# A three-stage graph network kernel: the root term of layer one moves from the prologue into the tiles of pass one, and the step tables are turned before they are written

## The chip, the cores and the metric

The kernel runs on one core of a Trainium2 chip. The metric is the device time of one execution in microseconds (us); lower is better. Engines are named as in the profile: PE is TensorE, DVE is VectorE, ACT is ScalarE, POOL is GpSimd, SP is SyncE. The names ending in q (SPq, ACTq) are an engine's own sequencer, here the rows in which it issues transfers.

## What is computed

There are 12500 nodes with rows of 128 floats and 400000 edges, sorted by destination. Cut to what matters:

```python
h = relu(layernorm(x))
# relational convolution, 10 relations, applied twice
def rgcn(h, w_rel, root, bias):
    mean = segment_sum(h[src], dst * 10 + edge_type) / max(count, 1)   # (N, 10, 128)
    return einsum('nrd,rdo->no', mean, w_rel) + h @ root + bias
x = x + rgcn(relu(rgcn(h, w_rel1, root1, b1)), w_rel2, root2, b2)
# attention of four heads over the same edges
h = relu(layernorm(x))
x = x + attention(h, src, dst, W_l, W_r, att, bias)
```

`edge_type` is the position of the largest of ten of the 42 attributes of an edge. The term `h @ root1 + b1` is called the root term of layer one below.

## The kernel before, in words

The program has four stages with a barrier of all engines after each of the first three: `prologue()`, pass one (`rgcn_pass("p1", True, NextRows)`), pass two (`rgcn_pass("p2", False, Attention)`) and `attention_pass()`. Nothing of a stage starts before the one ahead of it has ended on every engine.

**The prologue** works through the nodes in 15 blocks (`NB`), each of 7 tiles (`BT`) of 120 nodes (`TN`). For block b, ACT issues the load of x (420 KB) into one of two buffers (line 494), DVE takes mean and variance (`stats`, lines 376 to 386), ACT takes the root (503), DVE the inverse (`inverse`, 388 to 394), ACT writes seven normalized tiles (`rows`, 505 to 514), and SP stores them to the table `htab[0]` (line 328, 433 KB), which the gathers of pass one read. PE then turns the seven tiles (`turn`), multiplies each by `root1` and adds `b1` by a product of one row of ones (`product`, lines 571 to 580); ACT copies the turned tiles out of PSUM (`turned`) and the products into `A_all` (`out_rows`). Each engine takes its blocks in a fixed order that is written out by hand, so whatever stands in one block's turn on an engine delays the next block there.

Into the same blocks other work is set. DVE's `more(b)` (lines 448 to 474) runs after `inverse(b)` and ahead of `stats(b + 2)`: casts in blocks 1 and 2, `last_rows` in 3, three rounds of counting in 4, 5 and 6 (`counted`: 14, 9 and 6 passes over 625 numbers that PE has spread over the partitions, `spread`), the step tables in 7 (`tables`), and one quarter of the edge types of the first two chunks of edges in each of blocks 8 to 11 (`rels.part`). The attributes for the last two of these are loaded by SP in blocks 9 and 10 (lines 330 to 332); each such load is 1.3 MB in two transfers (line 224). PE's order is: `turn(b)`, `product(b - 1)`, and behind these the early turning of destinations and sources in blocks 2 and 3 (line 588), `spread` in 4, 5 and 6 (lines 596 and 597), and `rels.turn` in 10 and 12.

After block 14, SP writes the step tables to memory. They lie in SBUF with one step per partition and are wanted in step order, so each four-byte number is an element of its own in these nine writes (lines 335 to 342):

```python
sp.dma_start(qstep_dram[0:QPLANE].rearrange("(c p) -> p c", p=P), qtab[:, :]).then_inc(s_step, 16)
```

Two more writes follow, SP waits for all eleven (line 345), and five reads bring the tables back in rows and spread over the partitions (lines 347 to 350); the last is 896 KB. Then the stage can end.

**Pass one and pass two** run the same function. POOL gathers the source rows of 625 groups of 640 edges, five indirect transfers for a group (line 700), into ten slots. 1680 steps in 168 rounds of ten each match one group with one window of 12 nodes: DVE builds the one-hot matrix (797), PE multiplies (919), DVE adds to the running sum (853), SP writes the sum out (756). From round 64 on each round also finishes one tile of 120 nodes. For tile n, SP reads ten partial sums into `S` (line 745, one at each step of the round), DVE waits for them at step 2 of the next round (line 807) and divides by the counts, PE turns ten blocks of 120 x 128 (882), DVE copies them out (832, parts of 4, 4 and 2 tiles), PE multiplies by the ten relation matrices (902) and DVE adds the result to `A_all` (825). There are 105 tiles. In pass one `NextRows` then makes the rows of layer two, with its own root product (991, 996, 997). Five late rounds at the end finish the last tiles with no steps beside them.

**The attention stage** gathers again for 625 groups and isn't touched by the change.

Of the kernel before, what the change touches and what calls it, by code (L numbers as in the profile page):

```python
# [20 lines left out]
I32 = mybir.dt.int32  # L21
# [84 lines left out]
def build(nc, x, src, dst, attr, w_rel1, root1, b1, w_rel2, root2, b2, w_l, w_r, att, bias, out,  # L106
# [78 lines left out]
    with outer:  # L185
# [78 lines left out]
        def prologue():  # L264

            with ExitStack() as st:
# [16 lines left out]
                tab = sbuf(st, "tab", [P, 5, SCOLS], I32)  # L283
                tabf = sbuf(st, "tabf", [P, SCOLS])
                qtab = sbuf(st, "qtab", [P, QCOLS], I32)
                qtabf = sbuf(st, "qtabf", [P, QCOLS])
                wtab = sbuf(st, "wtab", [P, WCOLS], I32)
                wt = sbuf(st, "t1_w", [P, D])
                brow = sbuf(st, "t1_b", [1, D])
                xin = [sbuf(st, f"t1_x{k}", [TN, BT * D]) for k in range(2)]  # L290
# [4 lines left out]
                ht = [sbuf(st, f"t1_ht{k}", [P, 4 * TN]) for k in range(2)]  # L295
# [3 lines left out]
                pt = [bank[:, 1024 + k * 512:1024 + k * 512 + 4 * TN] for k in range(2)]  # L299
                py = [bank[0:TN, 2048 + k * 512:2560 + k * 512] for k in range(2)]  # L300
# [8 lines left out]
                s_eps, s_w = sem("t1_eps_set", True), sem("t1_w_in", True)  # L309
                s_x = [sem(f"t1_x_in{k}", True) for k in range(2)]  # L310
                s_st, s_var, s_std, s_rs = sem("t1_stats", True), sem("t1_variance", True), sem("t1_std", True), sem("t1_rstd", True)
                s_hn, s_t, s_ht = sem("t1_rows", True), sem("t1_turned", True), sem("t1_copied", True)
                s_m, s_y = sem("t1_product", True), sem("t1_out", True)
                s_out = [sem(f"t1_stored{k}", True) for k in range(2)]

                with nc.Block() as block:

                    @block.sync
                    def _(sp):
# [14 lines left out]
                        with nc.allow_non_contiguous_dma(reason="a column per 128 steps"):  # L334
                            sp.dma_start(qstep_dram[0:QPLANE].rearrange("(c p) -> p c", p=P), qtab[:, :]).then_inc(s_step, 16)
                            sp.dma_start(qstep_dram[QPLANE:].rearrange("(c p) -> p c", p=P), wtab[:, :]).then_inc(s_step, 16)
                            sp.dma_start(qbase_dram.rearrange("(c p) -> p c", p=P), qtabf[:, :]).then_inc(s_step, 16)
                            sp.dma_start(base_dram.rearrange("(c p) -> p c", p=P), tabf[:, :]).then_inc(s_step, 16)
                            sp.dma_start(attcol_dram.rearrange("(c p) -> p c", p=P), tab[:, 4, :]).then_inc(s_step, 16)
                            for k in range(4):  # L340
                                plane = step_dram[1].rearrange("s k -> (s k)")[k * PLANE:(k + 1) * PLANE]
                                sp.dma_start(plane.rearrange("(c p) -> p c", p=P), tab[:, k, :]).then_inc(s_step, 16)
                        sp.dma_start(qdone, done_q).then_inc(s_step, 16)
                        sp.dma_start(done_dram.rearrange("(a g) -> a g", a=1), done_t[:, :]).then_inc(s_step, 16)
                        sp.wait_ge(s_step, 176)
                        for k, to in enumerate((qgroup, qlast)):
                            sp.dma_start(to, qstep_dram[k * QPLANE:k * QPLANE + to.shape[1]].rearrange("(a s) -> a s", a=1)).then_inc(s_step, 16)
                        sp.dma_start(attcol, attcol_dram.rearrange("(a s) -> a s", a=1)).then_inc(s_step, 16)
                        sp.dma_start(base[:, :], base_dram.rearrange("(a s) -> a s", a=1).to_broadcast([P, PLANE])).then_inc(s_step, 16)
                        sp.dma_start(qbase[:, :], qbase_dram.rearrange("(a s) -> a s", a=1).to_broadcast([P, QPLANE])).then_inc(s_step, 16)  # L350
                        sp.wait_ge(s_step, 256)
                        for k in range(2):
                            sp.wait_ge(s_out[k], 16 * ((NB + 1 - k) // 2))

# [12 lines left out]
                    def _(dve):  # L367
# [8 lines left out]
                        def stats(b):  # L376

                            k = b % 2
                            dve.wait_ge(s_x[k], 16 * (b // 2 + 1) + (16 if b == NB - 1 else 0))
                            if b >= 2:  # L380
                                dve.wait_ge(s_hn, b - 1)
                            for q in range(BT):
                                v.bn_stats(stat[k][:, q, :], xin[k][:, q * D:(q + 1) * D]).then_inc(s_st, 1)
# [40 lines left out]
                        def tables():  # L424

                            link(v.tensor_scalar(gs[:, :], gs[:, :], float(GROUPS - 1), None, ALU.min))
                            link(v.tensor_tensor(qtabf[:, :], snum[:, :], gs[:, :], ALU.subtract))
                            link(v.tensor_scalar(qtabf[:, :], qtabf[:, :], float(KW), None, ALU.mult))
# [1416 lines left out]
```

## Time and profile before

| | us |
|---|---|
| median of 3 runs | 12420.08 |
| lowest and highest | 12411.02, 12423.86 |
| profiled execution, its own time | 12413.02 |
| its span, first to last instruction | 12411.2 |

| engine | busy us | share of the span |
|---|---|---|
| PE | 9026.6 | 73% |
| PEld | 8216.0 | 66% |
| DVE | 7740.8 | 62% |
| ACT | 2071.1 | 17% |
| POOL | 8996.3 | 72% |

The shares are averages over four stages. The stages are told apart by POOL: it gathers in the two passes and in the attention stage, and stands still in the prologue and around each barrier. A duration such as "2.80" beside x7 is that of seven instructions merged into one row. PE's rows count the pieces of a product: a float32 product of two matrices is two records.

### The profile page before, as it was taken

What the parts mean: (1) busy time and instruction counts of PE and PEld (TensorE: products, weight loads), DVE (VectorE), ACT (ScalarE), POOL (GpSimd) and SP (SyncE); (2) the same over time, 40 slices, a digit from 0 to 9 for tenths busy, and PEclk for the clock granted to TensorE, in tenths of its full rate; (3) what the DMA queues carried; (4) which work ended last, traced back from release to release, by engine and by line L of the source; (5) the groups of instructions that cost most, each with busy time, mean ns of one, the idle gap of its engine ahead of it and who ended that gap; (6) DMA issues with size and microseconds to landing.
All of it is one profiled execution on the core that took longest, in us unless ns stands there. A gap on an engine that the chain in (4) does not pass through costs nothing. (4 is left out here: it accounts for less than half of the span.)

```text
span 12411.2 us, 236943 instructions
## 1 busy us (share of the span) xinstructions
PE 9026.6 (73%) x59599; PEld 8216.0 (66%) x59599; DVE 7740.8 (62%) x17428; ACT 2071.1 (17%) x5955; POOL 8996.3 (72%) x9486
## 2 busy tenths in 40 slices
PE   5566667777777766666777777766777777777777
PEld 4566667777777666666777777765666666666666
DVE  2555545666666655544777777764666667666677
ACT  2000000000000000000000000014444444444442
POOL 0677777777777677777777777757777777777776
PEclk6777888889889888888899899888988999999998
DMA  3666545555555444444555555557888888888887
GB/s 70 136 137 138 111 82 112 114 114 114 113 113 115 101 82 81 82 82 88 115 117 117 116 116 117 117 114 194 237 234 237 233 237 236 235 236 234 235 236 206
DMA packets 1434213, 1831.89 MB, mean 148 GB/s; under 512 B 379591, under 2 KB 998431, under 8 KB 1426692
## 3 DMA queue, kind: packets, MB, share of 16 engines
q0 software_dynamic: 300000, 634.20, 28.0%
q1 hardware_dynamic: 910830, 881.77, 26.6%
q10 hardware_dynamic: 222113, 300.75, 7.8%
q8 instruction: 581, 9.52, 0.3%
q14 instruction: 689, 5.64, 0.2%
HBM read 1355.30 MB, written 458.67 MB: 146 GB/s over the span
## 5 line engine op out<-in xcount | busy, mean ns | idle before, releaser
L700 POOL DMA_INDIRECT p_g<-htab,p_i x6250 | 5915.8, 947 | 1966.7 <-issue 1890.8
L919 PE MATMUL p_pg<-p_g,p_oh 128*120 x33600 | 4855.1, 309 | 1828.1 <-ACTq L726 1497.1
L919 PEld LDWEIGHTS p_pg<-p_g,p_oh 128*120 128x120 f32 x33600 | 4596.0, 214 | 2052.6 <-issue 2035.5
L1293 POOL DMA_INDIRECT a_g<-xlw,a_i x3125 | 2987.3, 956 | 1036.0 <-issue 876.1
L797 DVE SCALAR_TENSOR_TENSOR p_oh<-key,qbase,p_cols 128x600 f32<-128x600 f32 x3370 | 2800.8, 831 | 13.9 <-issue 13.9
L853 DVE SCALAR_TENSOR_TENSOR p_acc<-p_acc,cont,p_pg 120x129 f32<-120x129 f32 x3360 | 1165.8, 347 | 2591.3 <-PE p_pg L919 2370.0
L717 ACT ACTIVATE p_i<-src_i 128x5 int32<-128x5 int32 x1240 | 258.2, 208 | 7566.4 <-DMA p_g<-htab,p_i 6934.4
L1766 PE MATMUL a_px<-a_g,ident 128*128 x1450 | 736.2, 593 | 832.2 <-SPq L1348 784.0
L1755 PE MATMUL a_pg<-a_v,a_into 128*128 128x132 f32 x7000 | 974.0, 289 | 63.0 <-POOL a_v L1312 20.7
L1755 PEld LDWEIGHTS a_pg<-a_v,a_into 128*128 128x128 f32 x7000 | 908.2, 203 | 74.1 <-issue 36.3
L1766 PEld LDWEIGHTS a_px<-a_g,ident 128*128 128x128 f32 x1450 | 239.8, 207 | 913.8 <-issue 912.4
L1680 DVE TENSOR_TENSOR A<-a_pg,A 128x132 f32 x700 | 201.9, 288 | 942.6 <-PE a_pg L1755 910.0
L1772 PEld LDWEIGHTS a_px<-a_xr,a_onto 128*128 128x128 f32 x4350 | 715.9, 222 | 69.3
L1398 ACT ACTIVATE a_away<-a_dst,a_minus 128x640 f32 x727 | 602.8, 829 | 856.0 <-issue 328.9
L1689 DVE TENSOR_TENSOR a_relu<-a_relu,a_pcon 128x640 f32<-128x640 f32 x725 | 587.2, 810 | 251.4 <-ACT a_relu L1452 250.7
L1772 PE MATMUL a_px<-a_xr,a_onto 128*128 128x132 f32 x4350 | 713.9, 308 | 0.0
L1691 DVE TENSOR_REDUCE a_score<-a_relu 128x20 f32<-128x640 f32 x725 | 594.4, 820 | 25.1
L1451 ACT ACTIVATE a_relu<-a_px 128x384 f32<-128x384 f32 x725 | 352.5, 486 | 1457.5 <-PE a_py L1772 1444.8
L1531 DVE TENSOR_TENSOR a_into<-a_pcon,local 128x640 f32<-128x640 f32 x725 | 587.9, 811 | 8.0 <-issue 7.5
L1523 DVE TENSOR_TENSOR a_v<-a_xj,a_w 128x640 f32<-128x640 f32 x676 | 547.5, 810 | 70.3 <-issue 35.7
L902 PE MATMUL p_pt<-p_w,p_st 128*120 128x128 f32 x4200 | 533.8, 286 | 71.6 <-DVE p_st L832 71.6
L902 PEld LDWEIGHTS p_pt<-p_w,p_st 128*120 128x120 f32 x4200 | 510.4, 195 | 82.6 <-DVE p_st L832 81.9
(230 smaller groups left out, 7055.4 us busy)
## 6 DMA issues: line engine op xcount, KB each, us to landing
a_xj<-xjw ACTq DMA_DIRECT2D x725, 330.0 KB
xjw<-a_g SPq DMA_DIRECT2D x625, 330.0 KB
partial<-p_acc SPq DMA_DIRECT2D x3360, 60.5 KB
a_dst<-in_dst_dram SPq DMA_DIRECT2D x625, 320.0 KB
p_s<-partial SPq DMA_DIRECT2D x2100, 60.5 KB
p_g<-htab,p_i POOLq DMA_INDIRECT x6250
a_g<-xlw,a_i POOLq DMA_INDIRECT x3125
a_xr<-xrw ACTq DMA_DIRECT2D x728, 66.0 KB
```

The lines of the kernel that those rows point to most:

```text
L700: pool.indirect_dma_start(gath[:, (k * G + q) * W:(k * G + q + 1) * W], None, table, bass.IndirectOffsetOnAxis(ap=stage[k][:, q:q + 1], ax ...
L797: v.scalar_tensor_tensor(onehot[k][:, :].rearrange("p (t n) -> p t n", t=G), key_f[:, ds(within(gp1 * G - G, TILES - G), G)].rearrange("p ...
L853: v.scalar_tensor_tensor(acc[k][:, :], acc[(k - 1) % ALOOK][:, :], cont[0:KW, ds(s, 1)], pg[bank(c, k)], ALU.mult, ALU.add).then_inc(s_acc, 1)
L902: last = t.matmul(po, St[:, r * TN:(r + 1) * TN], wrel[:, r * D:(r + 1) * D], start=(r == 0), stop=(r == NREL - 1))
L919: last = t.matmul(pg[bank(c, k)], onehot[b][:, q * KW:(q + 1) * KW], gath[:, ds(to + q * W, W1)], start=(q == 0), stop=(q == G - 1))
L1293: pool.indirect_dma_start(gbuf[k][:, q * W:(q + 1) * W], None, xlw, bass.IndirectOffsetOnAxis(ap=stage[k][:, q:q + 1], axis=0)).then_inc(s ...
L1398: a.activation(away[:, :], dall[:, ds(at, GE)], ACT.Abs, bias=minus[:, ds(s, 1)]).then_inc(s_away, 1)
L1531: v.tensor_tensor(into[b][:, :].rearrange("p (t n) -> p t n", t=G), colp.rearrange("p (a n) -> p a n", a=1).to_broadcast([P, G, P]), local ...
L1691: v.tensor_reduce(score[at[0]][:, at[1] * G * H:(at[1] + 1) * G * H], L[to][:, :].rearrange("p (t c) -> p t c", c=C), AX, ALU.add).then_in ...
L1755: last = t.matmul(sums(j, b), into[b][:, q * P:(q + 1) * P], V[b][:, q * W:(q + 1) * W], start=(q == 0), stop=(q == G - 1))
L1766: t.matmul(px[b], ident[:, :], gath[:, ds(ring, HEADT * W)], start=True, stop=False)
L1772: last = t.matmul(to, onto[b][:, q * P:(q + 1) * P], xr[k % RING][:, :], start=False, stop=q in (HEADT - 1, G - 1))
```

## The change

- The prologue no longer turns its tiles, multiplies by `root1` or writes `A_all`. ACT, PE and their waits for each other in this work are gone (`turn`, `product`, `turned`, `out_rows`).
- PE's order in the prologue is now a plain list: the early turns, three times `spread`, the turning of the tables, two times `rels.turn`. ACT copies the early turns out after blocks 1 and 2 (2 and 3 before).
- x has three buffers in place of two. The first three loads are issued at the start, and the load of block b + 3 after `rows(b)`.
- All tables are made as float32 side by side in one tile `made` of 128 x 73. PE turns it once, DVE copies it out twice (as integers and as floats), and SP writes nine pieces with 512 bytes in a row each.
- These writes (`tables_out`) stand in SP's order after block 11's store, and the reads back (`tables_in`) after block 13's store. The attribute loads stand after the stores of blocks 10 and 11 in place of 9 and 10.
- In pass one each tile reads its own 120 rows of `htab[0]` (61 KB, one more transfer on SP, ahead of the ten), turns them as an eleventh block, and adds an eleventh product and the product of ones with `b1`. DVE's third copy is 360 columns wide in place of 240, its wait covers eleven transfers, and it copies the result to `A_all` in place of adding. `root1` and `b1` are loaded at the start of the pass. Pass two is as before.

The diff, cut to its core:

```diff
-                xin = [sbuf(st, f"t1_x{k}", [TN, BT * D]) for k in range(2)]
+                widths = (QCOLS, WCOLS, SCOLS, SCOLS, SCOLS, SCOLS, SCOLS, QCOLS, SCOLS)
+                starts = [sum(widths[:n]) for n in range(len(widths) + 1)]
+                made = sbuf(st, "made", [P, starts[-1]])
+                qtab, wtab, tab0, tab1, tab2, tab3, tab4, qtabf, tabf = (made[:, a:a + n] for a, n in zip(starts, widths))
+                lying_i = sbuf(st, "lying_i", [starts[-1], P], I32)
+                lying_f = sbuf(st, "lying_f", [starts[-1], P])
+                xin = [sbuf(st, f"t1_x{k}", [TN, BT * D]) for k in range(3)]
...
+                    def tables_out(sp):
+
+                        planes = step_dram[1].rearrange("s k -> (s k)")
+                        to = [qstep_dram[0:QPLANE], qstep_dram[QPLANE:], *(planes[k * PLANE:(k + 1) * PLANE] for k in range(4)),
+                              attcol_dram, qbase_dram, base_dram]
+                        sp.wait_ge(s_tab, 1)
+                        for n, one in enumerate(to):
+                            lying = lying_i if n < 7 else lying_f
+                            sp.dma_start(one.rearrange("(c p) -> c p", p=P), lying[starts[n]:starts[n + 1], :]).then_inc(s_step, 16)
+                        sp.dma_start(qdone, done_q).then_inc(s_step, 16)
+                        sp.dma_start(done_dram.rearrange("(a g) -> a g", a=1), done_t[:, :]).then_inc(s_step, 16)
...
-                            if b in (9, 10):
-                                sp.wait_ge(rels.s_used, b - 8)
-                                rels.fetch(sp, 1, b - 9)
-                        sp.wait_ge(s_tab, 1)
...
+                            if b in (10, 11):
+                                sp.wait_ge(rels.s_used, b - 9)
+                                rels.fetch(sp, 1, b - 10)
+                            if b == 11:
+                                tables_out(sp)
+                            if b == 13:
+                                tables_in(sp)
...
-                            v.engine_nop().then_inc(s_tab, 1)
+                            v.engine_nop().then_inc(s_seen, 1)
+                            dve.wait_ge(s_lie, 1)
+                            v.tensor_copy(lying_i[:, :], plying)
+                            v.tensor_copy(lying_f[:, :], plying).then_inc(s_tab, 1)
...
-                            k = b % 2
+                            k = b % 3
...
-                            if b >= 2:
-                                act.wait_ge(s_hn, b - 1)
+                            if b >= 3:
+                                act.wait_ge(s_hn, b - 2)
...
-                                act.wait_ge(s_t, 2 * (b - 1))
                                 act.wait_ge(s_out[k], 16 * (b // 2))
...
-                        for b in range(NB + 2):
-                            if b < NB:
-                                deviation(b)
-                                rows(b)
-                                if b + 2 < NB:
-                                    load_x(b + 2)
-                            if 1 <= b <= NB:
-                                turned(2 * b - 2)
-                                turned(2 * b - 1)
-                            if b >= 2:
-                                out_rows(2 * b - 4)
-                                out_rows(2 * b - 3)
+                        for b in range(NB):
+                            deviation(b)
+                            rows(b)
+                            if b + 3 < NB:
+                                load_x(b + 3)
+                            if b == 1:
+                                early_out(dst_f, 0)
                             if b == 2:
-                                early_out(dst_f, 0)
-                            if b == 3:
                                 early_out(src_i, len(early))
...
+                        pe.wait_ge(s_cast, 1)
+                        turn_early(dstc, 0)
+                        pe.wait_ge(s_cast, 2)
+                        turn_early(srcc, len(early))
+                        spread(0, finq)
+                        spread(1, lastw)
+                        spread(2, fint)
+                        pe.wait_ge(s_seen, 4)
+                        nc.tensor.transpose(plying, made[:, :], ident[:, :]).then_inc(s_lie, 1)
+                        pe.wait_ge(s_pa, 2 * len(early))
+                        rels.turn(pe, 0)
+                        rels.turn(pe, 1)
...
+                parts = NREL + (1 if first else 0)
...
+                        if first:
+                            sp.dma_start(wrel[:, NREL * D:], root1).then_inc(s_w, 16)
+                            sp.dma_start(brow, b1.rearrange("(a d) -> a d", a=1)).then_inc(s_w, 16)
...
+                            if k == 0 and first:
+                                sp.dma_start(own[odd], table[ds(n * TN, TN), 0:D]).then_inc(s_sr[odd], 16)
...
-                                gate(dve, "dve", (s_sr[odd], 16 * WT * half + 16 * WT))
+                                gate(dve, "dve", (s_sr[odd], 16 * parts * half + 16 * parts))
...
-                                v.tensor_tensor(to, to, po, ALU.add).then_inc(s_add, 1)
+                                if first:
+                                    v.tensor_copy(to, po).then_inc(s_add, 1)
+                                else:
+                                    v.tensor_tensor(to, to, po, ALU.add).then_inc(s_add, 1)
...
-                                for r in range(NREL):
-                                    last = t.matmul(po, St[:, r * TN:(r + 1) * TN], wrel[:, r * D:(r + 1) * D], start=(r == 0), stop=(r == NREL - 1))
+                                for r in range(parts):
+                                    last = t.matmul(po, St[:, r * TN:(r + 1) * TN], wrel[:, r * D:(r + 1) * D], start=(r == 0), stop=(r == NREL - 1 and not first))
+                                if first:
+                                    last = t.matmul(po, then.ones[0:1, 0:TN], brow, start=False, stop=True)
```

## Rows read from the trace of the kernel before

**Rows 1.** Timeline of POOL: first and last gather of pass one, first of pass two.
```profile
337.02 2.14 POOL L700 DMA_INDIRECT p_g<-htab,p_i  x1 [0.97 <-ACT p_i L713]
...
4252.38 0.95 POOL L700 DMA_INDIRECT p_g<-htab,p_i  x1 [0.30 <-issue]
4315.18 2.03 POOL L700 DMA_INDIRECT p_g<-htab,p_i  x1 [61.85 <-ACT p_i L713]
```

**Rows 2.** Waits of POOL, 330 to 4300 us: total us, times, longest us.
```profile
POOL p_g L700 <- ACT p_i L717: 7.9, 26, 0.3
```

**Rows 3.** Groups by line, prologue (0 to 336 us): busy us, mean ns, idle before.
```profile
L579 PE MATMUL t_psum<-t_b,ones 1*120 1x128 f32 x210 | 81.6, 490 | 0.0
L578 PE MATMUL t_psum<-t_w,t_ht 128*120 128x128 f32 x210 | 80.1, 485 | 1.2 <-ACT A L527 1.2
```

**Rows 4.** Timelines of ACT, PE and DVE in the prologue, put in order of time.
```profile
55.40 2.80 ACT L512 ACTIVATE t_h<-t_x,t_rs 120x128 f32<-120x128 f32 x7 [19.96 <-DMA htab<-t_h]
...
77.42 0.47 DVE L399 TENSOR_SCALAR key<-key 1x625 int32<-1x625 int32 x1
...
82.13 0.47 DVE L407 TENSOR_SCALAR done_t<-cont 1x625 int32<-1x625 f32 x1
...
92.77 5.11 PE L588 MATMUL t_psum<-ident,raw 125*128 125x125 f32 x24
...
116.83 0.87 DVE L414 TENSOR_SCALAR_CACHE_REDUCE qbase<-t_psum,snum 128x625 f32<-128x625 f32 x1 [17.48 <-PE t_psum L597]
...
129.68 1.46 DVE L383 BATCH_NORM_STATS2 t_st<-t_x 120x6 f32<-120x128 f32 x7
...
132.06 2.80 ACT L512 ACTIVATE t_h<-t_x,t_rs 120x128 f32<-120x128 f32 x7 [27.40 <-DVE t_rs L393]
...
185.44 0.17 DVE L426 TENSOR_SCALAR gs<-gs 128x14 f32<-128x14 f32 x1
...
194.69 0.17 DVE L445 TENSOR_SCALAR tab<-ring 128x6 int32<-128x6 f32 x1
...
197.28 0.82 DVE L237 TENSOR_REDUCE local<-local 125x64 f32<-125x640 f32 x1
...
200.86 0.20 DVE L248 TENSOR_SCALAR local<-local 125x64 f32<-125x64 f32 x1
...
211.18 0.36 ACTq L494 DMA_DIRECT2D t_x<-in_x_dram  x1
...
222.02 1.45 DVE L383 BATCH_NORM_STATS2 t_st<-t_x 120x6 f32<-120x128 f32 x7 [9.86 <-DMA t_x<-in_x_dram]
...
276.74 2.80 ACT L512 ACTIVATE t_h<-t_x,t_rs 120x128 f32<-120x128 f32 x7 [12.92 <-DVE t_rs L393]
...
281.86 2.80 ACT L512 ACTIVATE t_h<-t_x,t_rs 120x128 f32<-120x128 f32 x7 [0.47 <-DVE t_rs L393]
```

**Rows 5.** Timeline of SP's issues at the end of the prologue: start, us.
```profile
285.05 0.53 SPq L335 DMA_DIRECT2D qstep_dram<-qtab  x1
...
313.73 0.41 SPq L344 DMA_DIRECT2D done_dram<-done_t  x1
327.01 0.51 SPq L347 DMA_DIRECT2D tabs<-qstep_dram  x2
...
328.24 0.43 SPq L350 DMA_DIRECT2D qbase<-qbase_dram  x1
```

**Rows 6.** Windows: PE, PEld, DVE, ACT, POOL busy, PEclk, DMA share, GB/s.
```profile
80.00:100.00 20.00, 16.65 (x60) 12.22 (x60) 4.87 (x21) 6.58 (x15) 0.00 (x0) 1.00 0.18 44
100.00:132.00 32.00, 13.40 (x39) 9.03 (x39) 14.52 (x44) 4.17 (x11) 0.00 (x0) 0.51 0.11 27
```

**Rows 7.** Groups by line in the rounds with tiles, 2000 to 3600 us.
```profile
L902 PE MATMUL p_pt<-p_w,p_st 128*120 128x128 f32 x1380 | 176.2, 287 | 0.0
...
L882 PE MATMUL p_pt<-ident,p_s 120*128 120x120 f32 x680 | 103.7, 287 | 88.1 <-DVE A L825 52.8 <-DVE p_st L832 35.3
```

**Rows 8.** Waits of PE in the same stretch: total us, times, longest us.
```profile
PE p_pg L919 <- ACTq L726: 211.8, 126, 4.8
```

More of the change, by code:

```diff
@@ L298, in prologue @@
                 psf = bank[:, 0:1024]
-                pt = [bank[:, 1024 + k * 512:1024 + k * 512 + 4 * TN] for k in range(2)]
-                py = [bank[0:TN, 2048 + k * 512:2560 + k * 512] for k in range(2)]
+                plying = bank[0:starts[-1], 1024:1024 + P]
                 pz = [bank[:, 3072 + k * 512:3072 + k * 512 + 4 * CH] for k in range(2)]
@@ L343, in _ @@
[L343 to L348, printed above, removed]
@@ L378, in stats @@
                             k = b % 2
-                            dve.wait_ge(s_x[k], 16 * (b // 2 + 1) + (16 if b == NB - 1 else 0))
+                            dve.wait_ge(s_x[b % 3], 16 * (b // 3 + 1) + (16 if b == NB - 1 else 0))
                             if b >= 2:
@@ L559, in _ @@
                         t = nc.tensor
-                        def turn(p):
-                            b, n = p // 2, 4 if p % 2 == 0 else BT - 4
-                            pe.wait_ge(s_hn, b + 1)
-                            if p >= 2:
-                                pe.wait_ge(s_ht, p - 1)
-                            for q in range(n):
-                                at = 4 * (p % 2) + q
-                                last = t.transpose(pt[p % 2][:, q * TN:(q + 1) * TN], hb[b % 2][:, at * W:at * W + D], ident[0:TN, 0:TN])
-                            last.then_inc(s_t, 1)
-                        def product(p):
-                            n = 4 if p % 2 == 0 else BT - 4
-                            pe.wait_ge(s_ht, p + 1)
-                            if p >= 2:
-                                pe.wait_ge(s_y, p - 1)
-                            for q in range(n):
-                                to = py[p % 2][:, q * D:(q + 1) * D]
-                                t.matmul(to, ht[p % 2][:, q * TN:(q + 1) * TN], wt[:, :], start=True, stop=False)
-                                last = t.matmul(to, ones[0:1, 0:TN], brow[0:1, :], start=False, stop=True)
-                            last.then_inc(s_m, 1)
                         def turn_early(of, base_n):
@@ L881, in turn @@
                             for m, r in enumerate(which):
-                                last = t.transpose(to[:, m * TN:(m + 1) * TN], S[odd][:, r * W1:r * W1 + D], ident[0:TN, 0:TN])
+                                of = S[odd][:, r * W1:r * W1 + D] if r < NREL else own[odd]
+                                last = t.transpose(to[:, m * TN:(m + 1) * TN], of, ident[0:TN, 0:TN])
                             last.then_inc(s_t, 1)
@@ L894, in mean @@
                                 pe.wait_ge(s_cpy, 3 * n + 1)
-                                turn(odd, range(8, NREL), pT[0])
+                                turn(odd, range(8, parts), pT[0])
                             n, odd, half, here, later = tile_at(j, c, 2)
```

114 lines of the change are left out of this document (33 added, 81 removed).

## The prediction

> **What bounds the kernel now.** I first read POOL's timeline, because POOL alone tells the stages apart. Its first gather of pass one starts at 337.02 us, its last at 4252.38, and pass two's first at 4315.18 [rows 1]. Between the first two lie 3124 gathers, 1.25 us each. The waits say that nothing held POOL back in pass one: all its waits on ACT, which hands it free slots, come to 7.9 us, none over 0.3 [rows 2]. So pass one is bound by POOL's own pace, and whatever PE, DVE and SP do there is free as long as POOL isn't starved. The reader is to see a kernel of stages in series: a prologue of 337 us in which POOL stands still, a pass that POOL sets, and a tail of 4315.2 - 4253.3 = 61.9 us in which the last steps and tiles drain. Pass two and the attention stage aren't touched. The change can gain only in the first of these, and lose only in the second and third.
>
> Next the groups of the prologue. The root products take 210 and 210 records for 105 tiles, 81.6 + 80.1 = 161.7 us of PE [rows 3], 1.54 us a tile and 10.8 us a block of seven. They delay more than PE: the counting on DVE waited 17.48 us for a spread that stood behind them at 116.83 [rows 4]. Last the queue of SP. After block 14, nine writes of single numbers and two others run from 285.05 to 314.1, the reads back can start only at 327.01, and the first gather starts 10.0 us after that [rows 5, 1]. These 52 us are the prologue's end; both they and the PE work must go for the stage to get shorter.
>
> **Part one, the prologue.** With the products gone, its length is set by the hand-written order on DVE, ACT and SP. I follow it block by block with durations of before.
>
> The opening is bound by transfers: `rows(2)` started at 55.40, after 19.96 us of waiting for a store [rows 4]. The third load of x now stands beside these, 420 KB more; no row shows what it adds. Below: nothing, since it was loaded in that time anyway. Above: the 10.8 us that a load, a store and an attribute load took together (issued 211.18, used 222.02) [rows 4]. I take 2, as it is a fifth of those bytes: `rows(2)` from 57.4 to 60.2. Behind it ACT copies the turned sources out, as fast as PE turns them, 5.1 us (at 92.77) [rows 4], and only then takes the root of block 3. `inverse(3)` is at 66.5.
>
> From here DVE is the chain, because `more(b)` stands ahead of `stats(b + 2)`. One block's statistics and inverse take 132.06 - 129.68 = 2.4 us [rows 4]. `last_rows` takes 5.2 (82.13 + 0.47 - 77.42) [rows 4], giving 74.1 after the statistics. One pass of counting takes (129.68 - 116.83) / 14 = 0.92 us [rows 4]: 14, 9 and 6 of them are 12.9, 8.3 and 5.5 us, each with 2.4 behind it. The spreads run beside those 2.4 us. That is 74.1 + 26.7 + 7.2 = 108.0. The tables take 194.69 - 185.44 + 0.2 = 9.4 us [rows 4]. The new turn of 73 columns and two copies have no row; from below 0.3 (one turn and nothing else), from above a spread's 2.4 us with two handovers, 4; I take 1.5, nearest to a single turn and two small copies. With 2.4 behind: 121.3. A quarter of the edge types takes 200.86 - 197.28 + 0.2 = 3.8 us [rows 4]; blocks 8 and 9 end at 121.3 + 2 x 6.2 = 133.7, and `rows(10)` at 133.7 + 3.0 = 136.7.
>
> Now **two waits that weren't there**. The attributes for `more(10)` are issued after block 10's store, no longer a block ahead. DVE stands at them, with `stats(12)` and so `rows(11)` queued behind; SP's next store waits for that. The three transfers together took 10.8 us (211.18 to 222.02) [rows 4]. Each such block costs 10.8 + 3.8 + 2.4 + 3.0 = 20.0 us. Below, a transfer half as long makes it 15; above, 16 us of transfer makes it 25. `rows(12)` ends at 176.7. Block 13 adds 5.5 and block 14 the 5.1 us that lie between 276.74 and 281.86 [rows 4]: 182.2 and 187.3.
>
> The writes of the tables now stand ahead of block 12's store, eleven issues. The two that were rows already took some 0.4 us each (0.41 at 313.73) [rows 5], so some 5 us, beside DVE's second wait, where SP has nothing else to do; if that cover went, block 12's store would slip by them. The reads back are issued after block 13's store, at 182.5. Before, 10.0 us lay between their first issue and the first gather [rows 5, 1]; the last store now shares these, so 13. The last store itself, issued at 187.4, ends at about the same time. **The first gather starts at 195.5 in place of 337.0: -141.5 us.** PE's and ACT's other removed work is inside this; the two extra weight loads at the head of pass one lie ahead of no gather and cost nothing.
>
> One rule speaks against this part. The clock that was granted was 1.00 from 80 to 100 us and 0.51 from 100 to 132 [rows 6], so the lower clock came only late in the stage; I take full rate for the early turns and half for the spreads. The Trainium skill (TensorE: Matmul & The Clock Gate, "What's actually happening") says that half rate is the default and that activity releases it. By that rule the thinned-out PE would do the early turns at half rate, 5.1 us more, and the time would be 5 us above mine.
>
> **Part two, pass one.** Each tile gains one turn (103.7 / 680 = 0.15 us), one product (two records of 1380 in 176.2: 0.26) and one with the bias row, 0.26 again [rows 7]; at half rate that last is 0.78 (2 x 81.6 / 210) [rows 3]. So 0.7 us, at most 1.3, on PE, plus one issue on SP and a wider copy on DVE. A round is 3915 / 168 = 23.3 us, and PE waits for gathered groups 211.8 us in 1600, 3.1 a round [rows 8]. That idle time is the cover; 0.7 fits in it. If it were gone, 105 tiles would cost 74 us. In the tail there is no cover: five tiles finish behind the last gather at 0.7 us, **+3.5 us** (0 to 7). DVE's wait for eleven transfers in place of ten costs nothing, since the eleventh is issued first.
>
> **Sum.** 12413.0 - 141.5 + 3.5 = 12275.0 for the profiled execution. The median shown is 7.1 us above that execution, so on its footing 12282.1; I say 12282.
>
> **The rivals.**
> A, transfers take DVE's place. The opening is bound by them, three loads are pushed into it, and both attribute loads now stand exposed. If the opening slips by the full 10.8 and each attribute load by 10 more, the first gather is at 226 and the time 12313. For: DVE waited 9.86 us for x at 222.02 [rows 4]. Against: in 80 to 132 us the transfer engines were 11 to 18% busy [rows 6].
> B, the order hides less than I think: the blocks keep their pace because of some wait that I took for PE's, and only the prologue's end is cut. The nine writes fall away, 314 - 285 plus the 13 us to 327.01, some 42 us [rows 5]: 12420 - 42 = 12378. Against: the 17.48 us names PE.
> C, the tiles crowd pass one. PE's clock or the longer chain of turns and copies makes POOL wait now and then; half of the exposed 74 us gives 12319.
> D, **slower**: the tile's gate. DVE's wait at step 2 (line 807) also holds back the steps' sums and one-hots. If the eleventh transfer, or SP's queue with it, holds DVE up for more than the 3.1 us of slack plus 138 / 105 = 1.3, so 4.4 us a tile, the gain is lost. At 5.5 us it is 105 x 2.4 = 252 us: 12420 - 138 + 252 = 12534. For: one more issue on SP's queue, which also serves the sums. Against: no wait of DVE on a transfer stands among the long ones.
> E, the change doesn't do what it says, since DVE or transfers had their own reason for each wait: within 25 us of no change.
>
> **Chances.** Forecast 0.76, A 0.11, B 0.04, C 0.05, D 0.02, E 0.02. Faster by over 0.2% (25 us, about what can be told from no change) takes in the first four: 0.96; same 0.02; slower 0.02. The range: downwards both attribute waits at 15 us take 10 off, the opening at no cost 2, the tail 3.5, and the median's footing 7: 12260. Upwards the clock adds 5, the attribute waits 10, the tail 3.5, the tables' turn 2.5, and A and C reach up to 12320.
>
> **What would show it.** Right: first gather near 195; DVE waits of about 10 us before line 237 in blocks 10 and 11; no wait for PE longer than a spread; POOL's waits on ACT in pass one still below 20 us; 62 us of tail become 65. The prediction is wrong if the stretch from `rows(3)` to `rows(10)` isn't near 70 us, if a wait on x or a store takes over there, or if POOL shows gaps beyond 0.3 us in the tile rounds.

## The result, and the profile after

| | before | after |
|---|---|---|
| median | 12417.74 us (4 runs) | 12281.04 us (4 runs) |
| lowest, highest | 12411.02, 12423.86 | 12275.18, 12286.73 |
| profiled execution | 12413.02 | 12275.18 |

The ratio is 0.9891 (95% interval 0.988 to 0.9903): 136.7 us less. A later pair gave 0.9885 (0.9869 to 0.9902), 12276.59 against 12421.3. The forecast was 12282.

First POOL's timeline of the changed kernel (start, us, line, tile): the same three places as [rows 1].

```profile
195.41 2.13 POOL L653 DMA_INDIRECT p_g<-htab,p_i  x1 [0.98 <-ACT p_i L666]
...
4110.68 0.94 POOL L653 DMA_INDIRECT p_g<-htab,p_i  x1 [0.30 <-issue]
4178.97 2.04 POOL L653 DMA_INDIRECT p_g<-htab,p_i  x1 [67.34 <-ACT p_i L666]
```

The first gather comes 141.6 us sooner. From there to the last gather it is 3915.3 us, in the kernel before 3915.4. The idle time behind it is 67.3 us in place of 61.9. So the whole gain lies ahead of 195.41, and 5.5 us of it are given back in the tail. From pass two's first gather to the end it is 8094.4 us, 1.6 less than before, which the change doesn't explain. The sum, 141.6 + 0.1 - 5.5 + 1.6 = 137.8, is the difference of the two profiled executions.

The waits in the prologue, by the waiting instruction and what ended the wait: total us, times, longest. First DVE's two largest for a block in the kernel before (0 to 337 us), then the changed kernel (0 to 198 us).

```profile
DVE t_st L383 <- DMA t_x<-in_x_dram: 68.0, 9, 15.6
...
DVE qbase L414 <- PE t_psum L597: 52.4, 3, 17.5
```

```profile
ACT t_h L517 <- DVE t_rs L396: 81.8, 14, 17.3
...
ACT t_h L517 <- DMA htab<-t_h: 17.1, 1, 17.1
DVE t_st L386 <- ACT t_h L517: 15.4, 3, 9.7
DVE local L237 <- DMA local<-in_edge_attr_dram: 14.7, 1, 14.7
DVE local L237 <- DMA ea<-in_edge_attr_dram: 14.5, 1, 14.5
```

Three things are to be seen. DVE's three waits of 17.5 us for a spread (one of them stands in [rows 4]) have shrunk to 0.6 us in all. Its waits for x, 68.0 us before and more than the spreads cost, are down to 9.1, all of them ahead of 20 us; the prediction names only one of them (9.86 us). And two waits are there that the kernel before didn't have: DVE stands 14.7 and 14.5 us at the attribute loads of blocks 10 and 11. What they do to the rest shows in ACT's rows (line 517 is `rows(b)`), here blocks 9 to 14:

```profile
126.00 2.80 ACT L517 ACTIVATE t_h<-t_x,t_rs 120x128 f32<-120x128 f32 x7 [2.40 <-DVE t_rs L396]
...
132.12 2.80 ACT L517 ACTIVATE t_h<-t_x,t_rs 120x128 f32<-120x128 f32 x7 [2.52 <-DVE t_rs L396]
...
153.06 2.80 ACT L517 ACTIVATE t_h<-t_x,t_rs 120x128 f32<-120x128 f32 x7 [17.35 <-DVE t_rs L396]
...
173.57 2.80 ACT L517 ACTIVATE t_h<-t_x,t_rs 120x128 f32<-120x128 f32 x7 [16.30 <-DVE t_rs L396]
...
178.86 2.80 ACT L517 ACTIVATE t_h<-t_x,t_rs 120x128 f32<-120x128 f32 x7 [2.30 <-DVE t_rs L396]
...
182.32 2.80 ACT L517 ACTIVATE t_h<-t_x,t_rs 120x128 f32<-120x128 f32 x7 [0.47 <-DVE t_rs L396]
```

Blocks 9 and 10 are 6.1 us apart, the two behind the loads come 20.9 and 20.5 us after the block ahead of them. The end of SP's queue, the answer to [rows 5]: the writes take 4.6 us for eleven, issued at 158.69 beside DVE's second wait, and the reads back are out before the last store.

```profile
158.69 0.74 SPq L322 DMA_DIRECT2D qstep_dram<-lying_i  x2
...
162.85 0.41 SPq L324 DMA_DIRECT2D done_dram<-done_t  x1
...
182.05 1.49 SPq L330 DMA_DIRECT2D tabs<-qstep_dram  x2
...
184.64 0.42 SPq L333 DMA_DIRECT2D qbase<-qbase_dram  x1
185.14 0.40 SPq L345 DMA_DIRECT2D htab<-t_h  x1
```

In pass one, the rounds with tiles (1860 to 3460 us): the groups by line that answer to [rows 7], with the new own turn and the bias product, and the wait that answers to [rows 8].

```profile
L864 PE MATMUL p_pt<-p_w,p_st 128*120 128x128 f32 x1518 | 186.6, 281 | 0.0
...
L866 PE MATMUL p_pt<-local,y_ones 1*120 1x128 f32 x138 | 32.7, 316 | 0.0
...
L844 PE MATMUL p_pt<-ident,local 120*128 120x120 f32 x68 | 19.3, 284 | 0.0
```

```profile
PE p_pg L883 <- ACTq L679: 159.4, 93, 4.9
```

The root term's own records are 19.3 us for the turn, 186.6 / 11 = 17.0 for the product and 32.7 for the bias in 68 or 69 tiles, together 1.0 us a tile. PE waits for gathered groups 52.4 us less, 0.77 us a tile, so the term is paid out of that idle time. The two numbers aren't the same thing: the mean granted clock of the stretch was 0.92 here and 0.89 in the kernel before, and the step products, which the change doesn't touch, took 931.5 us of PE in place of 957.2. POOL's waits on ACT for slots in the pass are 7.0 us, where they were 7.9.

### The profile page after: what moved, and what is told of

It is laid out like the page before. It is cut to its first block and busy times, and to the rows that moved or that the text cites. A ratio compares the mean times of both kernels' runs of the same rounds, so it can differ in the third digit from the quotient of the medians.

```text
span 12273.4 us, 236908 instructions
## 1 busy us (share of the span) xinstructions
PE 8873.7 (72%) x59600; PEld 8089.9 (66%) x59600; DVE 7757.1 (63%) x17430; ACT 2044.9 (17%) x5895; POOL 8995.7 (73%) x9486
## 5 line engine op out<-in xcount | busy, mean ns | idle before, releaser
L883 PEld LDWEIGHTS p_pg<-p_g,p_oh 128*120 128x120 f32 x33600 | 4544.3, 212 | 2026.4 <-issue 1997.2
```

Of the source, the lines that this page charges most:

```text
L883: last = t.matmul(pg[bank(c, k)], onehot[b][:, q * KW:(q + 1) * KW], gath[:, ds(to + q * W, W1)], start=(q == 0), stop=(q == G - 1))
```

## The experiments

Twelve runs of eleven kernels (one of them the changed kernel itself), in three sets, most of them with a single execution. The sets ran on different chips. On the chips of the first two sets the kernel before took 15981.29 us (one run) and 15948.28 (13 runs, 15906.29 to 15972.13); on the third 12421.3 (7 runs), as at first. The last section shows where the difference lies. The prologue is the same on all of them to about 1.5 us, so that the start of the first gather can be compared across the sets; times and pass one only within one.

**The order of the attribute loads.** `fetch_back`:

```diff
-                            if b in (10, 11):
-                                sp.wait_ge(rels.s_used, b - 9)
-                                rels.fetch(sp, 1, b - 10)
+                            if b in (9, 10):
+                                sp.wait_ge(rels.s_used, b - 8)
+                                rels.fetch(sp, 1, b - 9)
```

> The changed kernel with the attribute loads of the second chunk back behind the stores of blocks 9 and 10 (10 and 11 in the changed kernel). In the changed kernel DVE stands 14.7 and 14.5 us at them and the first gather starts at 195.4 us. Theory (the chain is DVE's order, and these two waits are on it): the first load can be issued about 6 us sooner against its use and the second a whole block sooner; the waits fall to about 8 and 2 us and the first gather starts near 176. Rival (transfers bound this stretch, whatever their order): the time comes back as waits on x or on stores, and the first gather stays above 190.

First gather at 177.14, 18.3 us sooner. DVE's waits in the prologue of this kernel:

```profile
DVE local L237 <- DMA local<-in_edge_attr_dram: 8.6, 1, 8.6
...
DVE local L237 <- DMA ea<-in_edge_attr_dram: 2.0, 1, 2.0
```

The two waits fell by 6.1 and 12.5 us, together 18.6, and all of that reached the first gather. In this stretch the chain is DVE's order, and transfers had room.

**The third buffer.** `two_buffers`: `range(3)` to `range(2)`, `b % 3` to `b % 2`, and the load of block b + 2 after `rows(b)`.

> The changed kernel with two buffers for x in place of three, all else as it is. Theory: where blocks are short (8 to 10) a load needs 5 to 6 us between rows(b) and stats(b + 2), which the third buffer hides; each of these blocks grows from 6 to about 11 us, block 14 by 5, the opening by 2 to 5, and the first gather starts near 218 in place of 195.4. Rival (DVE's other work hides the loads): 195 to 200.

First gather at 217.60, 22.2 us later than in the changed kernel. From 20 us on DVE now waits for x, where in the changed kernel it didn't:

```profile
DVE t_st L386 <- DMA t_x<-in_x_dram: 60.7, 8, 16.3
```

Counted from the start it is 69.0 us, against the changed kernel's 9.1. So the third buffer is worth 22 us, once the products are out of the way.

**The turned tables.** `tables_in_columns`, at the new place in SP's order:

```diff
-                            sp.dma_start(one.rearrange("(c p) -> c p", p=P), lying[starts[n]:starts[n + 1], :]).then_inc(s_step, 16)
+                                sp.dma_start(one.rearrange("(c p) -> p c", p=P), of).then_inc(s_step, 16)
```

> The changed kernel with the nine table writes as before, one number an element, at their new place behind block 11's store. Theory: SP needs some 28 us to issue them in place of 4, so block 12's store is issued at about 187 in place of 176.4, and the reads back wait for the writes until about 200; the first gather starts at 211 to 215 (195.4 in the changed kernel). Rival 1 (at their new place the writes are hidden, and the turning brought nothing): 195 to 200. Rival 2 (they cost all that they cost before, 41 us): 236.

First gather at 211.94, 16.5 us later. SP's queue in this kernel:

```profile
161.63 12.62 SPq L325 DMA_DIRECT2D step_dram<-made_i  x4
...
188.94 5.93 SPq L348 DMA_DIRECT2D htab<-t_h  x2
200.50 0.52 SPq L333 DMA_DIRECT2D tabs<-qstep_dram  x2
```

The writes take SP from 157.58 to 188.9, block 12's store waits behind them, and the reads back start at 200.50. At their new place the element-wise writes cost 16.5 us. Behind block 14, 42.0 us lie between the first write and the first read back (285.05 to 327.01), and with turned tables at that same place 6.6 (285.66 to 292.30 in the next kernel), so that they cost 35.3 there. Moving them hides about half of that, turning them takes away the rest.

`tables_alone` is the kernel before with its tables turned, still behind block 14:

> The kernel before with only the tables turned by PE and written in rows, still behind block 14; two buffers, root term in the prologue. Theory (two paths end the old prologue almost together: the tables at 334.7 and the root products, whose last copy ends at 314.4): the tables' part falls from 52 to about 15 us, but the root products then end last, so that the first gather starts at 316 to 318 in place of 337, and the time is 20 us less (12398). Rival (the tables alone were the end): first gather at 302, 35 us less.

First gather at 317.01, 20.0 us sooner; median 15911.3 against 15948.28, ratio 0.9981 (0.997 to 0.9991). That is 37 us for the 20 forecast, with an interval of 14 to 48 us, so the total fits the theory and the rival alike, and only the first gather tells. SP read the tables back from 292.30 on, and then ACT's last copy of root products (line 530) held the stage:

```profile
293.52 0.43 SPq L349 DMA_DIRECT2D qbase<-qbase_dram  x1
315.87 0.40 SPq L742 DMA_DIRECT2D p_w<-in_L_gnn_w_rel_dram  x1
```

```profile
314.48 0.49 ACT L530 ACTIVATE A<-t_psum 120x384 f32<-120x384 f32 x1 [3.66 <-PE t_psum L582]
```

**The root term alone.** `root_alone` is the changed kernel with two buffers, the loads behind blocks 9 and 10, and element-wise writes behind block 14 (the edits above together, and `tables_out` and `tables_in` behind the loop).

> The changed kernel with two buffers, the attribute loads behind blocks 9 and 10, and the tables written number by number behind block 14: of the change only the move of the root term is left. Theory (the products held up DVE's counting and stood behind block 14, and the tables then end alone): block 14's rows end near 189, the tables' 52 us follow, first gather at 238 to 248 (337 before), pass one as in the changed kernel. With the tables alone the first gather came from 337 to 317. Rival (the two paths gate each other and the move alone brings little): first gather above 290.

First gather at 253.82, 83.2 us sooner than before, and 6 later than the upper end expected. Time 12332.73, ratio 0.9929 (0.9913 to 0.9946), 88.6 us less. Both sizes were off: DVE waited 59.0 us for x from 50 us on, and block 14's rows ended at 197.6 where 189 was expected; the writes and reads then took 56 us, not 52:

```profile
DVE t_st L387 <- DMA t_x<-in_x_dram: 59.0, 8, 15.2
```

```profile
194.78 2.80 ACT L517 ACTIVATE t_h<-t_x,t_rs 120x128 f32<-120x128 f32 x7 [0.47 <-DVE t_rs L397]
```

So of 141.6 us, the root term alone gives 83.2 and the turned tables alone 20.0. The other 38.4 are in neither. They hold the gain of the third buffer and of the tables' earlier place in SP's order, less the 18 us that the later attribute loads cost. How they split isn't shown: neither the third buffer nor the earlier place was tried on the kernel before, where DVE waited 68.0 us for x.

**The root term's price in pass one.** `no_root` takes the own rows, the eleventh turn and product and the bias out of the pass.

> The changed kernel without the root term in pass one: no own rows, no eleventh turn and product, no bias (the first layer's root term and bias are left out of the result). In the changed kernel pass one lasts 3915.3 us from first to last gather, and 67.3 us lie between the last gather's end and the first of pass two (61.9 before). Theory: the root term costs nothing under the gathers and all of the 5.4 us in the tail; gathers 3915, tail 62, first gather still at 195. Rival (the longer tail comes from where pass one now starts or from the clock, not from the root term): tail 65 or more.

It ran where the kernel before takes 15948 us: first gather 196.74, gathers to 5243.71, tail 102.4. There is no changed kernel on that chip beside it, so that this run can't price the root term; it only shows that the prologue doesn't depend on it (196.7 against 195.4 and 195.9).

`ten_more_products` and `twenty_more_products` put extra products ahead of a tile's eleven:

```diff
+                                for r in (list(range(NREL)) * 1 if first else []):
+                                    t.matmul(po, St[:, r * TN:(r + 1) * TN], wrel[:, r * D:(r + 1) * D], start=True, stop=True)
                                 for r in range(parts):
```

> The changed kernel with ten extra products of the same shapes ahead of the eleven of every tile of pass one (overwritten by them, so the result stays). They add 2.6 us of PE to a tile. Theory (PE's idle time of 2.5 to 3 us in a round of 23.3 is the cover): the gathers still take 3915 to 3935 us and POOL's waits on ACT stay small; the tail grows from 67 to about 80. Rival (the cover is thinner than PE's idle time, since waits between PE and DVE can't be filled): the gathers take over 4000 us.

> The same with twenty extra products, 5.2 us of PE a tile. Theory: 2.2 to 2.7 us of them find no cover, so that the gathers take 230 to 290 us longer (4145 to 4205 in place of 3915), and the tail is about 93. Rival (slots and look-ahead smooth it away): under 4000. Rival 2 (every product added counts in full): 4450.

On that chip the gathers took 5178 and 5416 us. From ten to twenty they grew by 238 us, 2.3 us a tile for 2.6 us of products: there was little cover left. (The ten products measure 2.4 us of PE a tile in the third set, not 2.6.) Against what ten should be held there was no base, so the first run decides nothing; the third set has one.

> The changed kernel itself, beside the kernel before, so that the earlier experiments have their base. Should the program take 15900 us and more here, as in the experiments so far, then pass one isn't bound by POOL's pace there (the two kernels without the root term in pass one took 5047 us from first to last gather, four with it 5082 to 5088), and the theory is: first gather 195 to 197, gathers 5085, total 100 to 115 us below the kernel before in place of 137. Should it take 12400, then as before: 137 us less. Rival (the gain doesn't depend on what bounds pass one): 137 in both cases.

> The changed kernel with ten extra products a tile in pass one, 2.6 us of PE each, once more beside the changed kernel itself. Where POOL bounds pass one (12400 us before): gathers 3915 to 3935 us, tail about 80. Where it doesn't (15900 us): as measured there, 5178 us against 5085, 0.9 us a tile, since not all of PE's idle time can be filled. Rival (the first experiment's 5178 was the chip's scatter): within 20 us of the changed kernel.

The third set ran where the kernel before takes 12421 us. `changed_again`: 12276.59 us (12273.35 to 12282.83), first gather 195.92, gathers until 4113.38, tail 72.8. What the expectation says of the chips with 15900 us stays untried. `ten_more_again`: 12364.0 us, first gather 196.92, gathers until 4142.05, tail 123.6. The waits of POOL, of `changed_again` first (1400 to 5000 us):

```profile
POOL p_g L653 <- ACT p_i L666: 72.8, 1, 72.8
POOL p_g L653 <- ACT p_i L670: 7.0, 23, 0.3
```

```profile
POOL p_g L653 <- ACT p_i L666: 123.6, 1, 123.6
POOL p_g L653 <- ACT p_i L670: 52.1, 81, 3.9
```

The expectation missed: I gave 3915 to 3935 us and a tail of 80, and it is 3945 and 124. Against `changed_again` the gathers grew by 27.6 us and the tail by 50.8. 370 records of the step products came after the last gather, against 180: PE had fallen behind by 19 steps, and the slots had let POOL run ahead. With ten more products PE's waits for groups fell from 153.5 us to 18.1 in 1600 us. Why the expectation missed is in the first of these numbers: 153.5 us in 68 tiles is 2.3 us a tile, and the ten products add 2.4 (158.4 us of PE in 66 tiles), so that the cover was too small even if all of it could be filled. (27.6 + 50.8) / 105 = 0.75 us a tile came through and 1.7 found cover; this is rough, since the two tails had unequal clocks (0.80 in `changed_again`, 0.90 here). When POOL began to wait is seen from two stretches of `ten_more_again`, 2600 to 3200 us and 3200 to 3800:

```profile
POOL p_g L653 <- ACT p_i L670: 5.2, 17, 0.3
```

```profile
POOL p_g L653 <- ACT p_i L670: 27.7, 30, 3.9
```

Up to 3200 us POOL kept its pace with no wait over 0.3 us, while PE was already falling behind: from 1860 to 3200 us it made 5547 records of step products, where `changed_again` made 5730, so that it was 18 steps behind. **In this one run the missing cover went into a backlog first, and so into a longer tail, and only late into gaps in the gathers.**

**A version that beats both.** The two moves of attribute loads, and the reads back one block sooner. `attributes_later` is the first move by itself:

```diff
-                        rels.fetch(sp, 0, 0)
...
-                        rels.fetch(sp, 0, 1)
...
+                            if b in (2, 3):
+                                rels.fetch(sp, 0, b - 2)
```

> The changed kernel with the attribute loads of the first chunk (2.6 MB) behind the stores of blocks 2 and 3 in place of the head of SP's queue. ACT waits 17.1 us for block 0's store before rows(2), which starts at 56.4. Theory (the opening is bound by bytes in SP's queue): rows(2) starts at 43 to 48 and the first gather some 10 us sooner, near 185. Rival (the opening is bound by the pieces of 512 bytes of destinations and sources, not by the attributes): rows(2) starts at 53 or later and the first gather at 192 or later.

First gather at 186.33, 9.1 us sooner, and `rows(2)` in its place:

```profile
46.81 2.80 ACT L517 ACTIVATE t_h<-t_x,t_rs 120x128 f32<-120x128 f32 x7 [12.43 <-DMA htab<-t_h]
```

46.81 against 56.39 in the changed kernel: the opening is bound by what stands ahead of block 0's store in SP's queue. The attributes are only a part of it. SP is still held for 19.84 us at the load of the sources in pieces of 512 bytes, which the rival names, and for 18.50 at the load of single destinations behind it:

```profile
21.07 18.50 SPq L340 DMA_DIRECT2D key<-in_dst_dram  x1
39.61 10.35 SPq L343 DMA_DIRECT2D htab<-t_h  x3
```

Block 0's store was issued at 39.61 in place of 47.97. What the opening would be without these two wasn't tried. `all_three` has all three moves:

> The changed kernel with three moves in SP's order: the attribute loads of the first chunk behind the stores of blocks 2 and 3, those of the second chunk behind the stores of blocks 9 and 10, and the reads back of the tables behind block 12's store in place of 13's. Alone, the first move brought the first gather from 195 to 186.3 and the second to 177.1. Theory (both are on one chain, so that they add, and the third takes 2 to 4 us off the end): first gather at 163 to 168, the time 27 to 32 us below the changed kernel. Rival (without its stalls the chain meets the transfers of x): first gather at 174 or later.

12245.04 us (12241.14 to 12249.13), ratio to the kernel before 0.9858 (0.9841 to 0.9874), and 31.6 us below the changed kernel beside it; the ranges of the two don't touch. First gather at 164.62:

```profile
DVE local L237 <- DMA local<-in_edge_attr_dram: 8.6, 1, 8.6
...
DVE t_st L386 <- DMA t_x<-in_x_dram: 6.4, 3, 4.8
```

Against 195.41 that is 30.8 us. The two moves of loads gave 9.1 and 18.3 by themselves; the 3.4 left over lie in the 2 to 4 expected of the reads back, which weren't moved alone. DVE's waits for x are 6.4 us, so none took the place of the others.

## Why the prediction was right, point by point

The time was forecast at 12282, and 12281.04 was measured. The steps, forecast and measured in the profiled execution:

| step | forecast | measured |
|---|---|---|
| start of `rows(2)` | 57.4 | 56.39 |
| end of `rows(10)` | 136.7 | 134.92 |
| a block behind an attribute load | 20.0 | 20.9, 20.5 |
| first read back of the tables | 182.5 | 182.05 |
| end of `rows(13)` | 182.2 | 181.66 |
| end of `rows(14)` | 187.3 | 185.12 |
| first gather | 195.5 | 195.41 |
| gathers of pass one | no change | 0.1 less |
| tail | +3.5 | +5.5 |

That the times agree so closely is partly luck. For the profiled execution 12275.0 was forecast and 12275.18 measured, and in it the tail is 2.0 us longer than forecast while the untouched stages happened to run 1.6 us shorter. In the prologue three steps came 1 to 2 us early, and the way from the last of them to the first gather took that much longer than forecast.

**That DVE's order is the chain** is shown for the attribute loads: `fetch_back` took 18.6 us out of two of its waits and 18.3 came through. For blocks 4 to 10 it is read from the trace: from 65.4 to 132 us all of DVE's waits come to 1.8 us. These attribute waits are 14.7 and 14.5 us, not the 10 that were named as the sign, because DVE comes to them some 3 us before the load is issued; the block's 20 us had this time in it. **Block 14** took 3.5 us, not 5.1: the 5.1 came from rows of the kernel before in which ACT copied turned tiles and products in between, the very work that the change removes. **The opening** came 1 us later than before, where 2 was taken (`rows(2)` 56.39 against 55.40). **The turning of the tables** cost 1.1 us (116.43 + 0.17 to the end of the second copy at 117.73), for which 1.5 was taken. **The attribute loads** took 11.7 and 11.2 us from issue to use, for 10.8.

**The pass.** 0.7 us a tile was forecast; the root term's records measure 1.0, inside the 1.3 given as the most. The product is 0.25 us for 0.26. The turn is 0.28 for 0.15 and the bias 0.47 for 0.26, since the rates were taken from the ten turns and the ten products of a tile. The trace of before had rows of the same shapes for both, the turn and the bias of layer two, at 0.27 and 0.54 us a tile (2000 to 3600 us):

```profile
L997 PE MATMUL p_pr<-y_b,y_ones 1*120 1x128 f32 x138 | 37.5, 356 | 0.0
...
L991 PE MATMUL p_pr<-ident,y_hn 120*128 120x120 f32 x68 | 18.3, 270 | 0.0
```

The prediction took all 3.1 us of a round's idle time as cover. `ten_more_again` fills nearly all of it and leaves 18.1 us in 66 tiles, 0.3 a tile. At 1.0 us the cover was ample, and rival C didn't come.

**The tail** was the term that was sized on thin ground. It is 67.3 and 72.8 us in two profiles of the same kernel, and 61.3 in `root_alone`, which has the same tiles. The windows of the tails (PE, PEld, DVE, ACT and POOL busy, PEclk, DMA share, GB/s) show what else moves it; first `changed_again`, then `root_alone`:

```profile
4113.00:4186.00 73.00, 58.99 (x373) 52.51 (x371) 39.10 (x86) 1.02 (x10) 0.39 (x1) 0.80 0.27 55
```

```profile
4169.00:4230.00 61.00, 46.13 (x368) 41.19 (x367) 38.01 (x84) 0.69 (x6) 0.19 (x1) 1.00 0.30 64
```

The granted clock was 0.80 in the one and 1.00 in the other; PE was busy 13 us longer for nearly the same number of records. With the two other profiles that have these tiles the tail goes with the clock: 61.3 us at 1.00, 67.3 at 0.86 (the changed kernel), 70.5 at 0.84 (`all_three`), 72.8 at 0.80. The kernel before had 61.9 us at 0.90. On a line between 61.3 and 67.3 the tail with the root term would be 65.6 us at 0.90, so that 3.7 of the +5.5 us would be the root term and 1.8 the clock that happened to be granted. That is an estimate; no pair of runs with equal clocks shows it.

**The rivals.** A (transfers take over) fell: the waits for x are 9.1 us, and a block behind an attribute load takes 20.9 and 20.5 us for the 20.0 forecast. B fell by the table above. D: DVE's wait at step 2 (line 766 now) names no transfer in the tile rounds. Of E nothing is left.

**The clock.** By the rule of the Trainium skill (TensorE: Matmul & The Clock Gate, "What's actually happening") the early turns would have run at half rate. The prediction took full rate for them, since the row of the granted clock has 1.00 up to 100 us [rows 6]. That reading was wrong: PE's own records don't follow this 1.00. In the kernel before a product with `root1` (line 578) has a mean of 484 ns up to 100 us and of 485 from 100 to 300, where the row says 0.50. In the changed kernel the row says 1.00 from 30 to 40 us:

```profile
30.00:40.00 10.00, 5.03 (x25) 3.87 (x25) 4.22 (x17) 3.88 (x8) 0.00 (x0) 1.00 0.36 108
```

But these are the groups of the early turns at 33 to 34.5 us, at 37.5 to 39, and at 60 to 62, where the row says 0.50:

```profile
L550 PE MATMUL t_psum<-ident,raw 125*128 125x125 f32 x5 | 1.3, 421 | 33.5 <-DVEq L459 33.5
```

```profile
L550 PE MATMUL t_psum<-ident,raw 125*128 125x125 f32 x7 | 1.3, 286 | 0.1
```

```profile
L550 PE MATMUL t_psum<-ident,raw 125*128 125x125 f32 x8 | 1.9, 422 | 8.7 <-ACT src_i L525 8.7
```

The first turns, after 33.5 us in which PE had done nothing, took 421 ns, as those at the lower level (1.2 GHz) did, and 286 ns a few turns later. So the trace agrees with the page. The 5.1 us that the prediction read from the kernel before were a duration with the lower level in it already (25 turns with a mean of 398 ns at 80 to 100 us), and nothing was left to be added: ACT's copies of the source turns took from 59.62 to 64.7, again 5.1 us. The forecast was right here for a wrong reason.

## What to carry to other kernels

Where stages stand in series behind barriers, add up the hand-written order of the short stage block by block: eight durations from the trace gave its end within 0.1 us, with errors of 1 to 2 us that cancelled. Take each duration from a row in which the work stands as it will stand after the change, with the same neighbours. Compare the mean length of PE's records before you believe the row of its clock at the head of a trace. Work on one path can delay another: with the root products gone, the rows of block 14 ended at 197.6 in place of 284.7, and the tables behind them started sooner without being touched (83 us), while turned tables alone gave 20, since the products then ended last. Look at what the freed stage waits for next; 31 us more lay in the order of four loads and of the reads back. When work is put under a bound engine, compare it with the idle time that is left, and watch the tail as well as the gaps: with ten more products here POOL kept its pace for long, and 50.8 of the 78.4 us came behind the last gather.

## What the runs showed that was not expected

On two of the chips the same program takes 15948 us in place of 12420. The prologue isn't slower (first gather 196.7 and 195.9 against 195.4), nor is one gather. In `no_root`, on such a chip, 2500 to 4500 us:

```profile
L653 POOL DMA_INDIRECT p_g<-htab,p_i x1190 | 1122.9, 944 | 878.4 <-ACT p_i L670 552.0 <-issue 326.3
```

POOL, at 944 ns a gather as everywhere, now waits 552 us for slots, and PE's timeline there has stretches in which products of one step stand apart, waiting for nothing that the profile shows:

```profile
3007.54 0.27 PE L876 MATMUL p_pg<-p_g,p_oh 128*120 x1 [0.97 <-issue]
3008.28 0.27 PE L876 MATMUL p_pg<-p_g,p_oh 128*120 x1 [0.47 <-issue]
```

Elsewhere in this trace, and on the other chips, such a step runs ten records in 1.36 us. These gaps are only a part: of PE's waits in these 2000 us the largest, 233.3 us, is for DVE's copies (line 788), and DVE in turn stands 576.7 us for something that the profile calls only "remote", which no wait of the changed kernel in 1860 to 3460 us names. The granted clock is 0.80, against 0.92 there. Pass one is slower by 29% to 30%, the written-out prologue isn't. No run here tests a cause, and it stays open. Also open is what the root term costs there: the two kernels without it in pass one took 5047 us, both on one chip, four with it 5082 to 5088, all on the other, and the chips can't be parted from the edit.
